# A slope constant, a copy in four pieces and three range-mark operations on another engine, in a top-64 gated cross-attention block on one Trainium2 core

## The reference

```python
Q = (q @ Wq.T + bq).reshape(b, h, s, d)          # h = 16, s = 256, d = 16
K = (k @ Wk.T + bk).reshape(b, h, s, d)
scores = jnp.einsum('bhqd,bhkd->bhqk', Q, K) / jnp.sqrt(jnp.asarray(d, Q.dtype))
topk_scores, topk_idx = jax.lax.top_k(scores, topk)       # topk = 64
probs = jax.nn.softmax(topk_scores, axis=-1)
...
x_q = (x.astype(jnp.float32) / s_in).astype(jnp.float8_e4m3fn)
...
x = x + jnp.tanh(g_xattn[0]) * _L0_xattn_ref(_layernorm(x, axis=-1), ctx_1024, ctx_1024, ...)
x = x + jnp.tanh(g_ffn[0]) * _L0_ffn_ref(_layernorm(x, axis=-1), ...)
```

## Time and profile before

| | |
|---|---|
| median of 3 runs | 3022.32 us (3021.08 to 3029.27) |
| profiled execution, its own time | 3019.36 us |
| its span, first to last instruction | 3017.5 us |
| DVE busy | 2564.5 us (85%) |
| ACT busy | 2500.6 us (83%) |
| PE busy, weight loads apart | 1434.2 us (48%) |
| POOL busy | 1007.2 us (33%) |
| mean granted TensorE clock | 0.66 |

### The profile page before, as it was taken

How to read it: one execution, slowest core, us unless ns; L and a number is a source line. 1 busy time by engine, 2 the same in 40 slices (tenths; PEclk the granted TensorE clock), 3 DMA queues, 4 the chain that set the end, 5 groups by cost and what they waited for, 6 DMA issues and landing times. The chain is left out here.

```text
span 3017.5 us, 56335 instructions
## 1 busy us (share of the span) xinstructions
PE 1434.2 (48%) x9104; PEld 920.2 (30%) x9104; DVE 2564.5 (85%) x10738; ACT 2500.6 (83%) x8774; POOL 1007.2 (33%) x1204
## 2 busy tenths in 40 slices
PE   3345555445544545433445445554445345445443
PEld 2123333333322333322333233332233233233321
DVE  1688899888989898888888889988988888898884
ACT  1679999799988899957989799998799699697982
POOL 5223343233434233422333334332343233232112
PEclk8556676666666776666766576766666676666656
DMA  4323333223333323232223333323233223232111
GB/s 69 48 39 64 61 57 59 49 57 63 68 57 52 62 57 63 55 54 42 54 56 66 57 65 56 63 57 61 53 61 64 44 52 63 46 65 44 36 37 33
DMA packets 451929, 166.76 MB, mean 55 GB/s; under 512 B 245616, under 2 KB 451440, under 8 KB 451520
## 3 DMA queue, kind: packets, MB, share of 16 engines
q1 hardware_dynamic: 451136, 162.38, 30.2%
q0 software_dynamic: 384, 0.33, 0.1%
HBM read 102.57 MB, written 59.24 MB: 54 GB/s over the span
## 5 line engine op out<-in xcount | busy, mean ns | idle before, releaser
L971 ACT ACTIVATE act_junk<-score_sb,X 128x256 int8<-128x256 f32 x3072 | 1522.1, 509 | 141.3 <-DVE X L1293 60.2
L971 ACT ACTIVATION_READ_ACCUMULATOR act_junk<-score_sb,X 128x1 f32 x3072 | 621.9, 202 | 0.0
L1006 ACT ACTIVATE unfit<-score_sb,thr 128x256 bf16<-128x256 f32 x1024 | 431.1, 514 | 169.5 <-DVEq L1444 169.5
L759 PE MATMUL ps_s<-ks,qs 96*128 96x256 bf16 x1024 | 231.8, 347 | 610.6 <-DVE score_sb L1179 600.6
L773 PE MATMUL ps_e<-qs,ks 99*128 99x256 bf16 x1024 | 348.9, 352 | 275.1 <-ACT unfit L1006 185.5
L1179 DVE TENSOR_SCALAR_CACHE_REDUCE score_sb<-ps_s 128x256 f32<-128x256 f32 x1024 | 397.9, 411 | 16.3 <-PE ps_s L759 10.8
L777 PE MATMUL ps_e<-dropb,unfit 128*128 128x128 bf16 x2048 | 350.4, 270 | 0.0
L1015 ACT ACTIVATE pT_sb<-ps_e 128x512 f32<-128x512 f32 x512 | 302.6, 592 | 51.6 <-PE ps_e L777 50.9
L794 PE MATMUL ps_o<-pT_sb,v_aug 128*32 128x256 f32 x2048 | 285.9, 499 | 110.2 <-ACT pT_sb L1015 59.2
L567 POOL CAST split<-proj 128x512 bf16<-128x512 f32 x64 | 46.5, 727 | 862.8 <-ACT proj L955 862.3
L1317 DVE TENSOR_SCALAR_CACHE_REDUCE masked<-score_sb,X 128x256 f32<-128x256 f32 x768 | 318.8, 470 | 13.9 <-DVE x_res L1497 8.4
(11 more groups left out here) (181 smaller groups left out, 3843.5 us busy)
## 6 DMA issues: line engine op xcount, KB each, us to landing
rows<-q_scr SPq DMA_DIRECT2D x192, 128.0 KB, 5.0
rows<-k_scr SPq DMA_DIRECT2D x192, 128.0 KB, 4.9
o_scr<-o_sb SPq DMA_DIRECT2D x128, 128.0 KB, 2.8
q_scr<-split SPq DMA_DIRECT2D x32, 384.0 KB, 2.7
k_scr<-split SPq DMA_DIRECT2D x32, 384.0 KB, 2.7
x_in<-in_x SPq DMA_DIRECT2D x32, 256.0 KB, 2.8
ctx_sb<-in_ctx SPq DMA_DIRECT2D x32, 256.0 KB, 3.0
v_scr<-proj SPq DMA_DIRECT2D x32, 256.0 KB, 5.9
```

What stands on the lines that cost most here:

```text
L759: ins = nc.tensor.matmul(ps_s[:, n % 2, jh * TOK:(jh + 1) * TOK], qs[u][0:SPLITS, h, 8 * jh:8 * jh + 8, :].rearrange("d j t -> d (j t)"), ...
L971: ins = nc.scalar.activation(act_junk[:, t % JUNK, :], score_sb[:, slot, t, :], ACT.Sign, scale=-1.0, bias=X[slot % 2][:, 0, t:t + 1], acc ...
L1006: ins = nc.scalar.activation(unfit[:, n % MASKS, jh, :], score_sb[:, slot, t, :], ACT.Relu, scale=-1.0, bias=thr[:, slot, t:t + 1])
```

## The change

Three things change. The constant SLOPE goes from 0.0115 / 2 to 0.0123 / 2. POOL's copy by head becomes four instructions, each with a quarter of the 16 blocks of features (96 x 1024 elements); the semaphore is raised by the last one only. The three mark operations leave `prepare_rounding` on DVE and stand at the end of `round_tokens` on POOL, each with a wait for the one before; a new semaphore, `s_nn`, tells `finish` that they are done, and `s_nan` now counts two steps an item in place of five.

```diff
-SLOPE = 0.0115 / 2
+SLOPE = 0.0123 / 2
...
+        s_nn = sem("range_marks_made")
...
-                nc.gpsimd.tensor_copy((qs, ks)[k][u][0:SPLITS].rearrange("d h j t -> d j h t"),
-                                      rows[:].rearrange("d j (h t) -> d j h t", t=D)).then_inc((s_qh, s_kh)[k], 1)
+                for j in range(0, NJ, NJ // 4):
+                    ins = nc.gpsimd.tensor_copy((qs, ks)[k][u][0:SPLITS, :, j:j + NJ // 4, :].rearrange("d h j t -> d j h t"),
+                                                rows[:, j:j + NJ // 4, :].rearrange("d j (h t) -> d j h t", t=D))
+                ins.then_inc((s_qh, s_kh)[k], 1)
...
                 nc.gpsimd.tensor_tensor(xq_sb[:], ysum_sb, magic_sb[:], ALU.subtract).then_inc(s_q, 1)
+                pool.wait_ge(s_nan, 2 * b + 2)
+                carry(pool)
+                nc.gpsimd.tensor_scalar(nanrow[:], rowmax[:], 464.0, 3.0e38, ALU.is_gt, ALU.mult).then_inc(s_nn, 1)
+                pool.wait_ge(s_nn, 3 * b + 1)
+                carry(pool)
+                nc.gpsimd.tensor_scalar(nanrow[:], nanrow[:], 3.0e38, None, ALU.mult).then_inc(s_nn, 1)
+                pool.wait_ge(s_nn, 3 * b + 2)
+                carry(pool)
+                nc.gpsimd.tensor_tensor(rowmax[:], nanrow[:], nanrow[:], ALU.subtract).then_inc(s_nn, 1)
...
-                dve.wait_ge(s_nan, 5 * b + 1)
+                dve.wait_ge(s_nan, 2 * b + 1)
                 nc.vector.tensor_reduce(rowmax[:], yabs_sb, AX.X, ALU.max).then_inc(s_nan, 1)
-                dve.wait_ge(s_nan, 5 * b + 2)
-                nc.vector.tensor_scalar(nanrow[:], rowmax[:], 464.0, 3.0e38, ALU.is_gt, ALU.mult).then_inc(s_nan, 1)
-                dve.wait_ge(s_nan, 5 * b + 3)
-                nc.vector.tensor_scalar(nanrow[:], nanrow[:], 3.0e38, None, ALU.mult).then_inc(s_nan, 1)
-                dve.wait_ge(s_nan, 5 * b + 4)
-                nc.vector.tensor_tensor(rowmax[:], nanrow[:], nanrow[:], ALU.subtract).then_inc(s_nan, 1)
+                dve.wait_ge(s_nan, 2 * b + 2)
 
             def finish(b, p, masked_free):
...
-                dve.wait_ge(s_nan, 5 * b + 5)
+                dve.wait_ge(s_nn, 3 * b + 3)
```

## The result

The changed kernel takes 2953.34 us, the median of 4 runs (2946.32 to 2954.98), against 3023.41 (3021.08 to 3029.27) for the kernel before on the same chip. The ratio is 0.9755, with a 95% interval of 0.9742 to 0.9769. The forecast was 2953 us. The sum came out right, but none of its three terms did: one was too large and two too small, and one of these, the marks, depends on another part of the change. The rest of the text is about that.

The account below looks back on a forecast made before the run. DVE was taken to set an item's length nearly all round, ACT one stretch, with selections on top. From 3019.4 us, 40 (slope), 20 (copies) and 8 (marks) give 2951, 2954 against the median; said 2953, range 2938 to 2968, wider 2915 to 2988.

Parts of the forecast that it names:

- What bounds the kernel: Per item: DVE sets the length nearly all round, except ACT from round 1's to round 2's update, first half.
- The slope: Selections: fewer unsure tiles with SLOPE 0.0123 / 2, 15 tiles in 12 halves becoming 11 in 11; 40 us less.
- so I expect 11 tiles in 11 halves: Selections: the replay finds 12 tiles in 12 halves, one an equal pair not selected in the trace, so 11.
- the same ones but one: Selections at 0.0115: the trace has the replay's 16 tiles except one row with equal 64th and 65th scores: 15.
- The copies: POOL's copies by head: waiting DVE instructions get in between pieces of about 1.0 us; 20 us less in all.
- the pattern of one copy: One copy of the queries: the update's second operation waits until 4.8 us instead of 5.53, gaining 0.7 us.
- The marks: Range marks moved to POOL: DVE gives up 1.68 us an item, of which 0.3 counts over 29 items; 8 us.
- ACT gets its threshold 1.68 us earlier and can use 0 to 0.57 of it: First half, between updates of rounds 0 and 1: only part of DVE's saving counts, as ACT's stretch follows.
- Only the selections count: Rival: gains of copies and marks are hidden or given back, so 2982 us; chance 2 in 10.
- DVE time counts in full at the marks: Rival: ACT's wait only shadows DVE's lateness, so the marks give 49 us in place of 8, 2912; 1 in 10.
- The copies give all that ACT's wait allows: Rival: the update's small operations slip through, so the copies give 54 us in place of 20, 2919; 1 in 10.
- Slower: Rival: the update's operations each wait for a whole piece; 3036 us at 1.7 us a piece; 1 in 30.

Follow-up runs that it names:

- the seven tiles: The changed kernel with SLOPE at 0.0127 / 2 in place of 0.0123 / 2: 2893.91 us, ratio 0.9581 to the kernel before.
- the second profile of before: The kernel before, without an edit, profiled once more: 3036.43 us in the one profiled execution, a span of 3034.5 us.

## Why the prediction was right, and which steps were not

The three parts, added in the order slope, copies, marks, move the span by 3017.5 - 2995.7 = 21.8, then 27.6, then 15.1 us, 64.5 together. The forecast had 40, 20 and 8, which is 68. The errors cancelled: that the sum came within 1 us of the result is luck. Split by the medians of the timed runs in place of the spans, the slope gave 26, the copies on top of it 29 and the marks 13.

**What bounds the kernel** held. The copies shortened ACT's wait of 2.03 us (a median of 1.96, then 0.66) and left DVE's at 1.85; the marks lengthened DVE's wait of 1.84 (to 2.58) and left ACT's at 2.04. So each part works at the hand-over that the forecast gave it, and each wait moved the way it was to. By how much was off: DVE's was to go above 3 us and reached 2.68 and 2.87, ACT's was to end near 1.3 and ended at 0.56. What the forecast had not was ACT's new wait for the denominators' DMA, 2.02 us in an item.

**The slope** was mis-sized by its count of tiles. The price of a tile was right: 10.0 to 12.4 us in single halves, 10.5 to 11.9 by the seven tiles. The step "so I expect 11 tiles in 11 halves" failed: there are 12 in 12, and the one too many, half 3, was not in the profile that the 15 were counted in. Take it off on both sides and the forecast holds: the slope alone against the second profile of before is 3034.5 - 2995.7 = 38.8, and on top of copies and marks 2988.5 - 2953.0 = 35.5. The step relied on the trace having "the same ones but one"; the missing one was noticed, but that one execution's count could differ from the next one's was not weighed. It is open why half 3 is selected in some executions. That it stays at all three slopes is what a row with equal 64th and 65th scores would do; a missed window would be likely to move with the slope. No run tried this.

**The copies** were mis-sized, 27.6 in place of 20, and the step was the pattern of one copy. The forecast had the update's second operation start at 4.8 us after the copy's start, for a gain of 0.7. It ended at 4.42, for a gain of 1.3, and 22 such copies would give 29. The pieces took 1.04 us in the median, as forecast (the first two of the copy shown took 1.24); the delays at the hand-overs between them were taken too long, by about 0.4 us up to the update's first operation and 0.15 more up to the second. That one DVE instruction gets in at each boundary, and the next waits for a whole piece, was right. The Trainium skill (SBUF — State Buffer, "Who interferes with whom") has the shared port pair as an exclusive lock, and says of DVE's two-port modes that whoever comes first holds it for the whole instruction. The traces agree, for maskings with two inputs as well: the masking that took 3.81 us ended 0.28 us behind the whole copy, and the three operations that met a piece in the changed kernel ended 0.27, 0.02 and 0.04 us behind that piece. What the forecast had as a loss of 2 us, a longer copy of the keys, is too small for these runs to tell: cut or whole, 2951.9 and 2952.83.

**The marks** had the right reason and an unstated condition. The step "ACT gets its threshold 1.68 us earlier and can use 0 to 0.57 of it" fits where the copies are in pieces: 8.5 and 14.0 us from read 6 to 58, against 8, which is 0.33 and 0.54 us for each of the 26 items there. With whole copies they gave 0.1 and 0.4. There the four-tile masking came to stand over the keys' copy and lost 13 us, and cutting the keys' copy alone brought 10.4 back. The forecast costed the marks "on POOL" by who waits for their data, and nobody did; it did not ask which DVE instruction would meet POOL's next long one. The term for the end was missing too: 68.2 to 61.9 us after the last read, 6.3 of the 15.1. It shows with the new slope alone (68.0 to 62.0 with whole copies); with the old one the marks left the end as it was, 76.4 against 76.2 and 80.1, and 76.2 against 74.0 on top of the copies. Why was not looked into.

**The rivals.** "Only the selections count" is out: copies and marks gave 42.7 of the 64.5. "DVE time counts in full at the marks" is out: DVE's wait grew. "The copies give all that ACT's wait allows", 54, is out at 28. "Slower" needed pieces of 1.5 us; they took 1.04, but eight pieces show its mechanism, 9 us slower with more boundaries in the update.

## What to carry to other kernels

Where two engines lock each other out, cut the long instruction, and count the other engine's instructions that will arrive while the pieces run: each one waits for up to a piece, so the cut pays for few long instructions and costs for many short ones on the critical path. An edit that moves work off a critical engine also moves what that engine meets on the shared port; try it together with the edit that shortens the blocks, as here the marks were worth nothing alone and 8.5 to 14 us with the pieces, between the same two reads. And where the work depends on the data, count it in more than one profile before its change is costed, and compare stretches between fixed points rather than whole times.

## What the runs showed of the hardware

- The selection of one half came in one execution of a program and stayed away in another, for 10.0 us. The cause was not found.
- Moving DVE's update 1.3 us ahead brought ACT to a DMA's landing that it had mostly not waited for: 49.4 us in 23 waits, where it had been 9.5 in 8.
- A DVE instruction with one input also waits for POOL's copy: L1270, a conversion of 128x32 to int32, took 0.96 us beside a piece, and 0.17 to 0.18 elsewhere.
- A piece of 512 elements took 668 ns and one of 1024 1158 ns on average (the queries' copies, waits for DVE in both). The estimate from these is that an instruction costs POOL about 2 x 668 - 1158 = 178 ns over its elements.
